# Value columns of half the recurrence units spread by DMA instead of TensorE, in units of two columns by two chunks

## The chip, the cores and the metric
The kernel runs on one core of one Trainium2 chip. A core has TensorE (PE, matrix products into PSUM), VectorE (DVE), ScalarE (ACT), GpSimd (POOL) and SyncE (SP, which here only issues DMAs). The metric is the time of one execution in microseconds, on the device; lower is better.

## The reference
The input is 32 sequences of 128 tokens of width 512. A cross-attention layer is followed by a layer with a linear recurrence (an RWKV block). The part that the change touches is the recurrence over tokens, with 32 heads of 16 keys by 16 values:

```
w = exp(-exp(time_decay + tanh(x5[1] @ decay_w1) @ decay_w2))    # per token, head and key
r, k, v = x5[3] @ Wr.T, x5[0] @ Wk.T, x5[2] @ Wv.T
def step(s, (r_t, k_t, v_t, w_t)):
    a = k_t[:, :, :, None] * v_t[:, :, None, :]                  # 16 x 16 per head
    out = einsum('bhk,bhkd->bhd', r_t, u * a + s)
    return a + w_t[:, :, :, None] * s, out
att = group_norm(outs) ; x = x + att * silu(x5[4] @ Wg.T) @ Wo.T
x = x + sigmoid(xr @ ffn_Wr.T) * (relu(xk @ ffn_Wk.T) ** 2 @ ffn_Wv.T)
```

## The kernel before
**Tiling.** Two sequences make a group of T = 256 tokens (NB = 2, L = 128), 16 groups. Width lies on partitions in 4 chunks of 128; in a chunk, a partition is one key of one of 8 heads. For each value column d (16 of them) the state of a chunk over all tokens is a row of 256 elements per partition. A unit is 4 such columns of one chunk, 128 x 1024 elements in one of four slots of the tile st; a group has 16 units, numbered by chunk.

**A unit's steps.** spread (PE, line 721): eight matmuls copy the unit's four value columns from the tiles v_hi and v_lo (v split into two float32r parts) to all 16 keys of each head, into the two-bank PSUM tile pair. outer (DVE, line 1226) multiplies it by kT into st, one token later. first (ACT, line 1031) puts the state before the first token into the element that outer leaves free. scan (DVE, line 1237) runs the recurrence, four scans of 256. weigh (DVE, line 1247) multiplies by rT. reduce (PE, line 744), for two units at a time, sums over the keys into bank 7; the bonus (line 729) is a matmul into the other half of that bank. readout (DVE, lines 1255 and 1257) adds both into att.

**Order.** Each engine is given its steps by a written order (PE_ORDER, ACT_ORDER, POOL_ORDER, DVE_ORDER) which it runs once per iteration; "+1" and "+2" mark steps that belong to the group one or two iterations back. So three groups are in work: attention and norms of one, projections and recurrence of the next, and group norm and feed-forward of the one before. low, low_rank, mix, tdecay, decay and proj_r, proj_k, proj_v, proj_g make w, r, k, v and the gate; the other PE steps are attention (score, turn_p, values, share, project) and feed-forward (ffn_k, ffn_r, ffn_v). PSUM has four further banks, used in a ring: the keys of the PE steps take them in turn, and a step waits until the bank's last reader has emptied it. Every engine executes its queue in order; a wait holds up all that stands behind it.

**SP.** turn(it) issues the loads and stores of an iteration in this order: load_c, load_s 0 and 1, store (two DMAs of 256 KB, after ffn_v), bring, load_s 2, save, load_m, load_x, load_t, load_s 3.

## Time and profile before

| | |
|---|---|
| median of 3 runs | 2274.32 us (2273.31 to 2276.19) |
| profiled execution | 2273.57 us |
| its span | 2271.8 us |
| PE / DVE / ACT / POOL busy, share of the span | 94% / 86% / 56% / 26% |
| mean granted TensorE clock | 0.97 |
| DMA moved | 69.88 MB, mean 31 GB/s |

The span is the time from the first to the last instruction of the profiled execution. Busy shares are means over the whole span, in which two iterations at either end have only part of the work; the rows below look into a steady iteration. A group of instructions is shown with its line, engine and operation, what it writes and reads, the count, the busy time in us and the mean duration of one in ns, and the idle time in front of it with its releaser.

### The profile page before, as it was taken

What the parts mean: (1) busy time and instruction counts of PE and PEld (TensorE: products, weight loads), DVE (VectorE), ACT (ScalarE), POOL (GpSimd) and SP (SyncE); (2) the same over time, 40 slices, a digit from 0 to 9 for tenths busy, and PEclk for the clock granted to TensorE, in tenths of its full rate; (3) what the DMA queues carried; (4) which work ended last, traced back from release to release, by engine and by line L of the source; (5) the groups of instructions that cost most, each with busy time, mean ns of one, the idle gap of its engine ahead of it and who ended that gap; (6) DMA issues with size and microseconds to landing.
All of it is one profiled execution on the core that took longest, in us unless ns stands there. A gap on an engine that the chain in (4) does not pass through costs nothing. (4 is left out here: it accounts for less than half of the span.)

```text
span 2271.8 us, 41733 instructions
## 1 busy us (share of the span) xinstructions
PE 2143.0 (94%) x14176; PEld 1477.1 (65%) x14176; DVE 1953.2 (86%) x4863; ACT 1260.9 (56%) x4405; POOL 585.4 (26%) x700
## 2 busy tenths in 40 slices
PE   7796999999999999999999999999999999999876
PEld 4574766667676666767667676766767676676533
DVE  2277989989898998989899898989989898998982
ACT  5555383845738384573838457383845738384312
POOL 1312232142223214222331422232142223314200
PEclk7898999999999999999999999999999999999977
DMA  8001001010010101001010100101010010100000
GB/s 282 31 20 31 2 11 50 11 50 11 16 35 11 50 11 50 11 16 36 11 50 11 50 11 14 38 11 50 11 50 11 11 41 11 50 2 29 1 19 10
DMA packets 48978, 69.88 MB, mean 31 GB/s; under 512 B 20512, under 2 KB 26656, under 8 KB 48768
## 3 DMA queue, kind: packets, MB, share of 16 engines
q1 hardware_dynamic: 48768, 67.21, 9.0%
q8 instruction: 115, 1.88, 0.4%
q14 instruction: 95, 0.78, 0.1%
HBM read 50.42 MB, written 16.78 MB: 30 GB/s over the span
## 5 line engine op out<-in xcount | busy, mean ns | idle before, releaser
L1237 DVE TENSOR_TENSOR_SCAN st<-ws,st 128x256 f32<-128x256 f32 x1024 | 637.7, 686 | 0.1
L866 ACT ACTIVATE probs_or_mixes<-probs_or_mixes,least 128x128 f32<-128x128 f32 x1024 | 399.0, 403 | 100.1 <-DVE least L1184 99.1
L1226 DVE TENSOR_TENSOR st<-bank_pair,kT 128x1016 f32<-128x1016 f32 x256 | 308.2, 1204 | 87.9 <-PE bank_pair L721 87.9
L1247 DVE TENSOR_TENSOR st<-st,rT 128x1024 f32<-128x1024 f32 x256 | 318.1, 1243 | 0.0
L1126 POOL TENSOR_SCALAR rstd<-rstd 128x1 f32<-128x1 f32 x96 | 26.6, 277 | 1099.9 <-ACT cin L899 599.9
L1184 DVE CUSTOM_DVE_ANT_0 probs_or_mixes<-bank,nmask 128x128 f32<-128x128 f32 x1024 | 231.2, 285 | 82.4 <-PE bank L568 76.8
L1120 POOL TENSOR_TENSOR probs_or_mixes<-probs_or_mixes 128x512 f32<-128x512 f32 x160 | 190.2, 1221 | 341.2 <-DVE probs_or_mixes L1278 341.2
L866 ACT ACTIVATION_READ_ACCUMULATOR probs_or_mixes<-probs_or_mixes,least 128x1 f32 x1024 | 206.7, 202 | 0.0
L721 PE MATMUL bank_pair<-v_hi,sel 32*128 32x256 f32 x1024 | 194.1, 340 | 10.6 <-DVE st L1226 10.4
L721 PE MATMUL bank_pair<-v_lo,sel 32*128 32x256 f32 x1024 | 166.8, 286 | 0.0
L721 PEld LDWEIGHTS bank_pair<-v_hi,sel 32*128 32x128 f32 x1024 | 114.4, 185 | 72.3 <-issue 35.4
L577 PE MATMUL bank<-consts,probs_or_mixes 128*128 128x128 f32 x1024 | 156.5, 285 | 3.1 <-DVE least L1184 1.5
L577 PEld LDWEIGHTS bank<-consts,probs_or_mixes 128*128 128x128 f32 x1024 | 115.8, 143 | 60.8 <-issue 38.9
L568 PE MATMUL bank<-kbd,inputs_turned 32*128 32x256 f32 x1024 | 149.5, 408 | 5.9 <-DVE least L1184 3.8
L744 PE MATMUL bank<-st,consts 128*32 128x256 f32 x2048 | 140.8, 393 | 13.7 <-DVE st L1247 13.6
L877 ACT ACTIVATE probs_or_mixes<-bank 128x512 f32<-128x512 f32 x256 | 148.9, 599 | 8.1 <-PE bank L587 4.7
L1278 DVE SCALAR_TENSOR_TENSOR probs_or_mixes<-bank,cols,probs_or_mixes 128x256 f32<-128x256 f32 x320 | 129.2, 471 | 12.2 <-PE bank L657 10.7
L613 PE MATMUL bank<-wo,probs_or_mixes 128*128 128x512 f32 x256 | 118.4, 605 | 14.2 <-DVE probs_or_mixes L1206 13.3
L1103 POOL TENSOR_TENSOR rk<-rT,kT 128x256 f32<-128x256 f32 x64 | 92.8, 1450 | 147.0 <-issue 138.9
L700 PE MATMUL bank<-probs_or_mixes,wr 128*128 128x256 f32 x512 | 119.8, 387 | 7.6 <-DVE probs_or_mixes L1278 7.5
L796 PE MATMUL bank<-last_stage,fk 128*128 128x256 f32 x512 | 120.1, 389 | 6.5 <-DVE last_stage L1339 6.5
L554 PE MATMUL bank<-inputs_turned,wq 128*128 128x256 f32 x512 | 118.5, 384 | 6.5 <-DVE least L1184 6.5
(150 smaller groups left out, 4214.3 us busy)
## 6 DMA issues: line engine op xcount, KB each, us to landing
inputs_turned<-in_ctx_turned SPq DMA_DIRECT2D x16, 512.0 KB, 3.5
inputs_turned<-in_x_turned SPq DMA_DIRECT2D x16, 512.0 KB, 4.4
xin<-in_x SPq DMA_DIRECT2D x16, 512.0 KB, 3.7
x<-xin SPq DMA_DIRECT2D x16, 512.0 KB, 4.1
keep<-x SPq DMA_DIRECT2D x16, 512.0 KB, 3.6
out<-keep SPq DMA_DIRECT2D x32, 256.0 KB, 2.0
nmask<-in_mask SPq DMA_DIRECT2D x16, 128.0 KB, 4.1
wo<-in_wo SPq DMA_DIRECT2D x2, 1024.0 KB, 12.4
```

Of the source, the lines that this page charges most:

```text
L568: last = mm(ps[m][0][:, ci * 2 * L:(ci + 1) * 2 * L], qT[r, 2 * cp + ci, b, :], kbd[r, b, :, :], start=True, stop=True)
L577: last = tr(ps[:, j * P:(j + 1) * P], pr[:, n % 4, j, :], ident)
L721: last = mm(pair[:, s, k * T:(k + 1) * T], sel[r, d % 4, :], part[r, c, :], start=part is v_hi, stop=part is v_lo)
L744: last = mm(ps[32 * (d // 4):32 * (d // 4) + 32, 0:T], ebase[:, o:o + 32], st[:, u % SLOTS, n * T:(n + 1) * T], start=m == 0 and k == 0, s ...
L866: last = fn(pr[:, n % 4, j, :], pr[:, n % 4, j, :], ACT.Exp, bias=least[:, n, j:j + 1], scale=-1.0, accum_out=rsum[:, n, j:j + 1])
L877: fn(pT[:, n % 4], ps[:].rearrange("p (j t) -> p j t", j=4), ACT.Copy).then_inc(free, 1)
L1120: tt(v, v, xnT[:, 2 * p:2 * p + 2, :, 1:], ALU.add).then_inc(mixed.sem, 1)
L1184: last = nc.vector.tensor_tensor_reduce(pr[:, n % 4, j, :], ps[:, j * P:(j + 1) * P], nmask[:, n // 8, :], 1.0, BIG, ALU.add, ALU.min, lea ...
L1226: tt(dst, src, over(kv, DU, 1), ALU.mult).then_inc(outer.sem, 1)
L1237: last = nc.vector.tensor_tensor_scan(v, ws[:, c].rearrange("p b t -> p (b t)"), v, 0.0, ALU.mult, ALU.add)
L1247: tt(v, v, over(rT[:, u // PER, :], DU, 1), ALU.mult).then_inc(weighed.sem, 1)
L1278: last = stt(out=x5[:, k % 4, c], in0=ps[:, q * T:(q + 1) * T].rearrange("p (b t) -> p b t", b=NB), scalar=col("maa", f * NC + c), in1=sx[ ...
```

## The change
A unit becomes two value columns of two chunks (again 128 x 1024 elements). UNIT_D now lists a pair of columns, eight units per pair of chunks. Units 0 to 7 (chunks 0 and 1) are spread by PE as before, in four matmuls of 512 columns. Units 8 to 15 (chunks 2 and 3) are spread by DMA: ScalarE copies that half of v as float32 to a new tile v_1, SP stores it to a DRAM tensor v_rows, and one DMA per unit reads 8 rows of 4 KB, each 16 times, straight into the unit's slot of st, one element to the right. outer then multiplies in place. Scans are two of 512 per unit; reduce works in four matmuls of 512 columns and keeps bank 7 for four steps; the bonus moves to the ring of banks. Bank 7 is freed by the new signal read_out. rk and the join of v_hi and v_lo on POOL are done for two chunks at once, the join for units 0 to 7 alone. SP gets a written order too, and the orders of all engines are new.

```diff
+HALF_T = 2 * T
+UNIT_D = [(4 * (w % 2) + w // 2, 8 + 4 * (w % 2) + w // 2) for w in range(2 * PER)]
+PITCH = DU * T + 4
+BY_PE = UNITS // 2
 PE_ORDER = """
+reduce.4+2 low_rank.0+1 reduce.5+2 key.0 tdecay.0+1 low_rank.2+1 value.0 proj_r.0+1 proj_v.0+1 proj_k.0+1 decay.0+1
+spread.0+1 reduce.6+2 decay.1+1 reduce.7+2 spread.1+1 query.0 var.0+2 proj_r.1+1 score.0 spread.2+1 rstd.0+2 query.1
...
+score.14 turn_p.11 project.0 turn_m.1+2 turn_p.12 reduce.3+1 values.2 flip.1 turn_p.13 turn_p.14 turn_p.15 share.1
+values.3 project.1 ffn_k.0+2 ffn_k.1+2 ffn_r.0+2 ffn_r.1+2 turn_n.0 turn_n.1 ffn_v.0+2 ffn_v.1+2 low.0
 """
 ACT_ORDER = """
+low.0+1 first.12+2 state.0+1 key.0 tdecay.0+1 state.1+1 first.13+2 first.14+2 proj_v.0+1 first.15+2 proj_k.0+1
...
 """
 DVE_ORDER = """
+scan.12+2 mix.2+1 mix.3+1 outer.13+2 value.0 scan.13+2 outer.14+2 outer.15+2 scan.14+2 weigh.12+2 proj_v.0+1
...
+inverse.0 scan.5+1 outer.6+1 weigh.4+1 scan.6+1 weigh.5+1 score.10 score.11 weigh.6+1 outer.7+1 score.12 score.13
+gather.0 scan.7+1 score.14 score.15 weigh.7+1 outer.8+1 outer.9+1 project.0 inverse.1 readout.0+1 shift2.0+2
+outer.10+1 gather.1 scan.8+1 outer.11+1 project.1 scan.9+1 scan.10+1 scan.11+1 weigh.8+1 weigh.9+1 shift.0 weigh.10+1
+ffn_v.0+2 weigh.11+1 ffn_v.1+2 mix.0 mix.1 outer.12+1
 """
+SP_ORDER = """
+load_c.0 load_s.0+1 load_s.1+1 save_v.1+2 spread.8+2 spread.9+2 load_m.0 spread.10+2 spread.11+2 save.0+1 load_x.0
+load_t.0 store.0+3 spread.12+2 spread.13+2 spread.14+2 spread.15+2 bring.0+2 load_s.2+1 load_s.3+1
+"""
...
+            def save_v(g, _):
+                wait(sp, outer.sem, outer.after(g, 0))
+                key = ("proj_v", 1)
+                sp.wait_ge(emptied[XB.of(key)], XB.through(key, g))
+                for half in range(2):
+                    sp.dma_start(v_rows[:, half], v_1[64 * half:64 * half + 64, :, :]
+                                 .rearrange("p c n -> p (c n)")).then_inc(v_saved.sem, 16)
...
+                sp.wait_ge(v_saved.sem, v_saved.after(g, 2))
+                wait(sp, summed.sem, summed.after(g, (u - SLOTS) // 2 + 1))
+                r = HC * UNIT_D[u % (2 * PER)][0]
+                src = v_rows[r:r + HC].rearrange("h s n -> h (s n)")
+                sp.dma_start(st[:, u % SLOTS, 1:DU * T + 1],
+                             src.unsqueeze(1).to_broadcast([HC, HD, DU * T])).then_inc(landed[u % SLOTS].sem, 16)
...
             def spread(g, u):
+                wait(pe, outer.sem, outer.after(g, u) if u else outer.after(g - 1, BY_PE))
+                for part in (v_hi, v_lo):
+                    for half in range(2):
+                        d = UNIT_D[w][half]
+                        r = slice(32 * (d // 4), 32 * (d // 4) + 32)
+                        last = mm(pair[:, half, :], sel[r, d % 4, :],
+                                  part[r, :, :].rearrange("p c n -> p (c n)"),
+                                  start=part is v_hi, stop=part is v_lo)
...
             def reduce(g, q):
+                p, m = q // PER, q % PER
                 if m == 0:
+                    wait(pe, read_out.sem, read_out.after(g, p))
+                if m == PER - 1:
+                    bonus(g, p)
...
+                for half in range(2):
                     for u in (2 * q, 2 * q + 1):
+                        r = 64 * half + 32 * (u % 2)
+                        last = mm(bank[7][r:r + 32, :], ebase[:, o:o + 32],
+                                  st[:, u % SLOTS, half * HALF_T:(half + 1) * HALF_T], start=m == 0, stop=m == PER - 1)
...
             def first_state(g, u):
+                if u < BY_PE:
+                    wait(act, summed.sem, summed.after(g, (u - SLOTS) // 2 + 1))
+                else:
+                    v_there(act, g, u)
...
             def outer_(g, u):
+                if u < BY_PE:
+                    wait(dve, summed.sem, summed.after(g, (u - SLOTS) // 2 + 1))
+                    dve.wait_ge(spreaded.sem, spreaded.after(g, u + 1))
+                    src = pair[:].rearrange("p s (r t) -> p s r t", t=L)[:, :, :, 0:L - 1]
+                else:
+                    v_there(dve, g, u)
+                    src = dst
...
             def scan(g, u):
+                for half in range(2):
+                    v = st[:, u % SLOTS, half * HALF_T:(half + 1) * HALF_T]
```

v_there waits for the landing of the unit's own DMA.

## Rows read from the trace of the kernel before

**Rows 1.** DVE in order of time, value's sum in two groups: start us, us, instruction.
```profile
253.13 0.47 DVE L1172 TENSOR_TENSOR vpad<-bank,rows 128x128 f32<-128x128 f32 x2
...
1976.90 0.47 DVE L1172 TENSOR_TENSOR vpad<-bank,rows 128x128 f32<-128x128 f32 x2
```
**Rows 2.** Stretch, length; busy PE, PEld, DVE, ACT, POOL; clock, DMA share, GB/s.
```profile
651.10:783.70 132.60, 130.81 (x885) 90.66 (x885) 121.64 (x305) 78.37 (x275) 36.30 (x44) 1.00 0.08 26
...
1976.90:2100.00 123.10, 119.54 (x793) 82.46 (x793) 112.14 (x291) 74.33 (x264) 33.48 (x41) 1.00 0.04 14
```
**Rows 3.** Waits from 651.1 to 1049: waiter, releaser, us, times, longest.
```profile
DVE st L1226 <- PE bank_pair L721: 16.1, 6, 4.9
```
**Rows 4.** Busy time of one line alone in a period: spread (721), then reduce (744).
```profile
651.10:783.70 132.60, 14.33 (x128) 10.55 (x128) 1.00 0.08 26
651.10:783.70 132.60, 8.54 (x128) 3.44 (x128) 1.00 0.08 26
```
**Rows 5.** PE in order of time: one spread and the step behind it.
```profile
737.38 0.38 PE L721 MATMUL bank_pair<-v_hi,sel 32*128 32x256 f32 x2
...
738.04 1.12 PE L804 MATMUL bank<-fr,last_stage 128*128 128x512 f32 x2
```
**Rows 6.** Groups of VectorE by line and form: busy us, mean ns, idle before.
```profile
L1237 DVE TENSOR_TENSOR_SCAN st<-ws,st 128x256 f32<-128x256 f32 x1024 | 637.7, 686 | 0.1
L1247 DVE TENSOR_TENSOR st<-st,rT 128x1024 f32<-128x1024 f32 x256 | 318.1, 1243 | 0.0
L1226 DVE TENSOR_TENSOR st<-bank_pair,kT 128x1016 f32<-128x1016 f32 x256 | 308.2, 1204 | 87.9 <-PE bank_pair L721 87.9
L1257 DVE TENSOR_TENSOR att<-bank,dg 128x256 f32<-128x256 f32 x64 | 27.2, 424 | 2.2
L1339 DVE SCALAR_TENSOR_TENSOR last_stage<-last_stage,cols 128x256 f32<-128x256 f32 x128 | 52.0, 478 | 10.4 <-ACT last_stage L1039 10.4
L1287 DVE TENSOR_TENSOR v_lo<-bank,v_hi 128x512 fp32r<-128x512 f32 x32 | 21.5, 672 | 6.8 <-ACT v_hi L983 6.7
```
**Rows 7.** DMA issues: queue, count, KB each, median us from issue to landing.
```profile
inputs_turned<-in_ctx_turned SPq DMA_DIRECT2D x16, 512.0 KB, 3.5
inputs_turned<-in_x_turned SPq DMA_DIRECT2D x16, 512.0 KB, 4.4
out<-keep SPq DMA_DIRECT2D x32, 256.0 KB, 2.0
wq<-in_wq SPq DMA_DIRECT2D x1, 1024.0 KB, 7.6
```
**Rows 8.** DVE in order of time, mix.0 and mix.1.
```profile
754.56 3.22 DVE L1278 SCALAR_TENSOR_TENSOR probs_or_mixes<-bank,cols,probs_or_mixes 128x256 f32<-128x256 f32 x8
```
**Rows 9.** SP's queue in order of time, the two stores of a group.
```profile
750.56 2.81 SPq L441 DMA_DIRECT2D out<-keep  x2
```
**Rows 10.** PE and ACT around the boundary, in order of time.
```profile
751.25 1.54 ACT L956 ACTIVATE th<-bank 32x256 f32<-32x256 f32 x4 [6.36 <-PE bank L643]
755.57 1.97 PE L533 MATMUL bank<-inputs_turned,wk 128*128 128x256 f32 x8
757.47 1.07 PE L744 MATMUL bank<-st,consts 128*32 128x256 f32 x16
...
760.19 0.38 PE L721 MATMUL bank_pair<-v_hi,sel 32*128 32x256 f32 x2
760.77 1.89 PE L657 MATMUL bank<-th,w2s 32*128 32x256 f32 x16
763.12 2.18 PE L700 MATMUL bank<-probs_or_mixes,wr 128*128 128x256 f32 x9 [0.46 <-DVE probs_or_mixes L1278]
```
**Rows 11.** PE alone by half microseconds: busy, clock, where it stood still early in the run.
```profile
149.50:150.00 0.50, 0.18 (x2) 1.00 0.00 0
...
152.50:153.00 0.50, 0.37 (x3) 0.89 0.04 16
...
159.50:160.00 0.50, 0.50 (x9) 0.78 0.00 0
```

More of the change, by code:

```diff
@@ L121 @@
 PE_ORDER = """
-reduce.4+2 spread.12+2 low_rank.0+1 spread.13+2 key.0 reduce.5+2 tdecay.0+1 spread.14+2 low_rank.2+1 proj_r.0+1
-spread.15+2 decay.0+1 proj_v.0+1 proj_k.0+1 spread.0+1 reduce.6+2 decay.1+1 value.0 spread.1+1 reduce.7+2 query.0
-spread.2+1 var.0+2 proj_r.1+1 score.0 rstd.0+2 query.1 score.2 spread.3+1 proj_g.0+1 proj_g.1+1 turn_p.0 turn_p.1
-turn_p.2 reduce.0+1 spread.4+1 score.4 out.0+2 turn_p.3 score.6 spread.5+1 turn_p.4 out.1+2 values.0 reduce.1+1
-turn_p.5 score.8 spread.6+1 proj_v.1+1 turn_p.6 flip.0 proj_k.1+1 turn_p.7 turn_m.0+2 score.10 share.0 spread.7+1
@@ L156 @@
-scan.7+1 inverse.1 project.0 weigh.7+1 outer.9+1 shift2.0+2 gather.1 scan.8+1 project.1 outer.10+1 readout.1+1
-weigh.8+1 scan.9+1 outer.11+1 weigh.9+1 scan.10+1 scan.11+1 shift.0 weigh.10+1 ffn_v.0+2 weigh.11+1 ffn_v.1+2
-"""
+scan.12+2 mix.2+1 mix.3+1 outer.13+2 value.0 scan.13+2 outer.14+2 outer.15+2 scan.14+2 weigh.12+2 proj_v.0+1
+weigh.13+2 scan.15+2 weigh.14+2 weigh.15+2 outer.0+1 mix.4+1 readout.1+2 outer.1+1 scan.0+1 var.0+2 score.0 outer.2+1
+score.1 groupnorm.0+2 scan.1+1 outer.3+1 score.2 weigh.0+1 proj_g.0+1 score.3 weigh.1+1 scan.2+1 proj_g.1+1 weigh.2+1
@@ L495, in _ @@
             for it in range(G + LATEST):
-                turn(it)
+                for name, n, late in SP_STEPS:
+                    g = it - late
+                    if known(g) and not (g == 0 and name in FIRST):
+                        does[name](g, n)
             sp.wait_ge(stored.sem, stored.after(G, 0))
@@ L705, in spread @@
             def spread(g, u):
-                c = u // PER
                 if first_group(g) and u == 0:
@@ L710, in spread @@
                     pe.wait_ge(sel_ready, 1)
-                if u % (2 * PER) == 0:
-                    key = ("proj_v", u // (2 * PER))
+                if u == 0:
+                    key = ("proj_v", 0)
                     pe.wait_ge(emptied[XB.of(key)], XB.through(key, g))
-                wait(pe, outer.sem, outer.after(g, u))
-                for k in range(2):
-                    for part in (v_hi, v_lo):
-                        for s in range(2):
-                            d = UNIT_D[u % PER][2 * s + k]
-                            r = slice(32 * (d // 4), 32 * (d // 4) + 32)
-                            last = mm(pair[:, s, k * T:(k + 1) * T], sel[r, d % 4, :], part[r, c, :],
-                                      start=part is v_hi, stop=part is v_lo)
@@ L731, in reduce, with bonus @@
+                last.then_inc(spreaded.sem, 1)
+            def bonus(g, p):
+                pe.wait_ge(rk_done.sem, rk_done.after(g, p + 1))
+                ps, full = y_bank(("bonus", p), g)
+                for q in range(2):
+                    last = mm(ps[:, q * T:(q + 1) * T], ublk[:, 2 * p + q, :], rk[:, q, :], start=True, stop=True)
+                last.then_inc(full, 1)
             def reduce(g, q):
-                m, c = q % 2, q // 2
+                p, m = q // PER, q % PER
                 if m == 0:
-                    bonus(g, c)
+                    wait(pe, read_out.sem, read_out.after(g, p))
+                if m == PER - 1:
+                    bonus(g, p)
@@ L1222, in outer_ @@
[L1222 to L1226 removed]
+                dst = st[:, u % SLOTS, 0:DU * T].rearrange("p (s r t) -> p s r t", s=2, t=L)[:, :, :, 1:]
```

252 lines of the change are left out of this document (115 added, 137 removed).

## The prediction

> **What bounds the kernel now.** I read the page's busy shares first, then the period, then the waits inside a period. A group's value projection is added up on VectorE at 253.13 us for one group and at 1976.90 us for the thirteenth after it [rows 1]: (1976.90 - 253.13) / 13 = 132.6 us per group, so the steady part decides. In such a period TensorE is busy for 130.8 of 132.6 us, VectorE for 121.6, ScalarE for 78.4, GpSimd for 36.3, and TensorE's granted clock is 1.00 [rows 2], its upper level, 2.4 GHz. TensorE idles 1.8 us per period. VectorE idles 11, and the longest of its waits is for TensorE: in three periods 16.1 us in front of the outer products, for the spread [rows 3]. So TensorE's queue is the bound, with VectorE 9 us behind it. A change is worth what it takes off TensorE, until VectorE or a chain of waits is the next.
>
> **TensorE, removed and reshaped.** Eight of sixteen spreads per group leave TensorE. By busy time the sixteen cost 14.33 us [rows 4], 0.90 each, but neighbours overlap. Start to start one costs less: its first matmul starts at 737.38 and the next step's at 738.04 [rows 5], 0.66 us. Eight fewer give 8 x 0.66 = 5.3 us; the busy time would give 7.2. I take 5.3, because the period is made of starts. The eight that stay are 4 matmuls of 512 columns instead of 8 of 256: the same columns, fewer starts. The eight old ones start some 0.08 us apart (0.66 / 8), the two halves still lie in different row strips, and I take 0.6 us per group off. If the halves did not overlap when wide, each would cost some 0.3 us more, 2.4 us per group. The sums over the key rows (line 744) cost 8.54 us per group for eight steps [rows 4]; four wide matmuls instead of eight narrow ones in four column strips, the same columns, I take 0.5 us off, bounds 0 and 1.5. The bonus keeps its matmuls and moves to every fourth sum. TensorE: 5.3 + 0.6 + 0.5 = 6.4 us per period off, bounds 3 and 10.
>
> **VectorE.** 64 scans of 256 become 32 of 512. A scan takes 686 ns, a plain product of the same size 424, one of 1024 1243 ns [rows 6]: the slope of the products is (1243 - 424) / 768 = 1.07 ns per element and their fixed part some 150 ns. With that fixed part a scan costs (686 - 150) / 256 = 2.1 ns per element, a wide one 1.22 us, and each pair saves one fixed part less the overlap of neighbours (637.7 us / 1024 = 623 ns against 686, 63 ns): some 90 ns, 32 x 0.09 = 2.9 us, bounds 0 and 4.8. The read-out is 4 products of 512 (0.67 each by the v_lo row) for 8 of 256 (0.42): 0.7 us less. One v_lo subtraction goes, 0.7. The outer product of a unit that DMA spreads reads st in SBUF instead of the PSUM pair, as the product with r does: 1243 x 1016 / 1024 for 1204 ns, 8 x 0.03 = 0.2 us more. VectorE: 4.1 us less, 117.5. That is still under TensorE's 130.8 - 6.4 = 124.4, so none of it shortens the period by itself; it pays for new waits. GpSimd joins half as much of v and ScalarE's copies only change their target; both have idle time for it.
>
> **DMA, added.** Per group 2 stores of 128 KB and 8 spreads of 512 KB come to 4.4 MB; the kernel moves 26 GB/s, 3.4 MB per period, with a DMA share of 0.08 [rows 2], so the share goes to some 0.18 and the volume is free. The latency is not: spread.u waits in SP's queue for the sum that frees its slot, and for everything ahead of it. A 512 KB load lands 3.5 to 4.4 us after issue, a 1024 KB one 7.6, a 256 KB store 2.0 [rows 7]. Per pair of units:
> - Units 8 and 9 need reduce.2 and the stores of v. On VectorE some ten steps, about 14 us, lie between weigh.5 and outer.8: hidden.
> - Units 10 and 11 need reduce.3, which needs weigh.7. Behind it come read-out and shift2 (8 products of 478 ns [rows 6], less their overlap some 3.4 us) before outer.10. About 1 us can show on VectorE, whose slack covers it: the next step that TensorE needs is the shift, which waits for the chain of norms, and the new order leaves it only three scans and two products before that.
> - Units 12 and 13 are the tight ones. On SP, spread.12 stands behind the store of the group before, which waits for the last step of ffn_v. In the trace the second of these stores is issued at about 753.0 and SP is free at 750.56 + 2.81 = 753.4 [rows 9]. On VectorE only mix.0 and mix.1, 3.2 us [rows 8], lie before outer.12. scan.12, and behind it mix.2 and mix.3, queue behind outer.12, and TensorE's value and proj_r need banks that mix.2 empties.
> - Units 14 and 15 follow in the same queue, while VectorE has mix.2, mix.3, value and a scan to do: hidden.
>
> **The boundary, step by step.** TensorE ends low at 751.2 and has a bonus, a sum and a spread as cover until tanh is done at 751.25 + 1.54 = 752.8 [rows 10]. The sum alone reaches 752.2: 0.6 us idle. Then, by [rows 10], low_rank.0 1.9, key 1.9, a sum and tdecay 2.7 (757.47 to 760.19), low_rank.2 1.9: 761.2 at value. VectorE ends mix.1 at about 757.2. spread.12 is issued at 753.4 with half a megabyte of stores ahead of it, of which the second is just out: 4.4 + 1.6 = 6.0 us, lands at 759.4. The bounds are 3.5 and 7.6 us, 756.9 and 761.0; I take 6.0 since it is the nearest row with the same bytes per partition plus most of the store's 2.0. Then outer.12 1.1, scan.12 2.3, first half of mix.2 0.9: 763.7, so TensorE idles 2.5 us where it idled 0.46 [rows 10]: 2.0 us more. By the bounds it is -0.4 and 3.6.
>
> **DMA engines.** Every load of the trace has 128 partitions as its outermost dimension; the spread's source has 8. The page "DMA: Bandwidth & Descriptors" of the Trainium skill (section on why a DMA increments its semaphore by 16) says that a transfer runs on the largest number of engines, at most 16, that divides the outermost dimension of both sides, which would be 8 here. By that rule each engine carries as much as in the 1024 KB row, and the period would end at 132.6 - 6.4 + 0.6 + 3.6 = 130.4 us, not 128.8, the whole near 2241 us. No row of before shows such a transfer.
>
> **The sum.** 132.6 - 6.4 + 0.6 + 2.0 = 128.8 us, 3.8 less. Fourteen periods from 121.8 to 1976.9 give 53 us. The next iteration, which still has TensorE at 119.5 of 123.1 us [rows 2], gives 3. The last 172 us run a chain of one group's tail, in which narrow steps and DMA latency exchange; I leave it at 0 (bounds -8 and +8). The profiled execution took 2273.57 us with a span of 2271.8; 2273.6 - 56 = 2217.6. The median of the runs is 0.7 above it: **2218 us**.
>
> **The rivals.**
> - **Landing is hidden, TensorE sheds more.** The overlap that I gave away in the spread comes back (7.2 + 0.6 + 0.5) and spread.12 lands by 758: 132.6 - 8.3 + 0.6 + 0.4 = 125.3 us; 14 x 7.3 + 5 = 107, 2167 us. If only the landing is early, 126.8, 2186. For it: the busy time of rows 4. Against it: the store ahead of spread.12. Chance 0.26 for both.
> - **The boundary lets the clock fall.** The trace has such a place in its first periods: TensorE stands still from about 149.7 to 152.6 us, and the granted clock is at 0.50, the lower level of 1.2 GHz, from 152.9 to 159.7 [rows 11], 6.8 us of which half are lost, 3.4 us. Landing after 7.6 us makes the gap at value 2.5 + 1.6 = 4.1 us, and in every period: 132.6 - 6.4 + 0.6 + 3.6 + 3.4 = 133.8 us, 14 x 1.2 + 1 = 18 us slower, 2292 us. It decides from a gap of at most 2.9 us, as in that stretch; my forecast has 2.5, so it is near. For it: SP's order and a source of 8 rows. Against it: key, tdecay and low_rank.2 keep TensorE busy right before. Chance 0.22, and if the clock falls in every second period only, the time is near 2265.
> - **The work does not leave TensorE.** If wide halves do not overlap (2.4 us back) and the landing takes 7.6 us, 132.6 - 4.0 + 0.6 + 3.6 = 132.8: no change, 2274. Chance 0.08.
>
> The page "TensorE: Matmul & The Clock Gate" (section on what is happening) says that an array left idle is let have half of its clock pulses, and the trace agrees, with 0.50 after the stop in rows 11; by that rule a long enough gap gives the second rival's 2292.
>
> **How the numbers follow.** Forecast 0.44 (2190 to 2245 for its own bounds), the rivals 0.26, 0.22, 0.08. The range takes in the first rival but for its far end and the second: 2160 to 2295. This kernel can be told from no change at about 0.2%, 4.5 us. Faster: 0.44 + 0.26 and a little of the others, 0.73; within: 0.07; slower: 0.20.
>
> **What will show it.** In a steady period: TensorE's busy time near 124 us; a spread with 4 matmuls some 0.6 us start to start; wide scans at about 1.2 us; DMA share about twice; VectorE's wait before the outer product naming a DMA at unit 12, of 2 to 3 us; the landing of the 512 KB spreads, 4.4 or 7.6; TensorE's wait at value and the granted clock behind it. The prediction is wrong if ScalarE, whose first.12 now waits for the landing ahead of key, holds up more than value, or if other DMA waits fall on TensorE's path.

## The result and the profile after

The change made the kernel slower: 2439.76 us (2435.67 to 2443.24, 4 runs) against 2274.02 beside it, ratio 1.0724, 95% interval 1.0712 to 1.0737. The sign of the prediction was wrong and the time lies 145 us above its range. The profiled execution took 2443.24 us, its span is 2441.0.

The page after: busy times; the groups that answer to [rows 6]; the DMAs (count, KB each, median us to landing, where there is one).
```profile
PE 2165.6 (89%) x11616; PEld 1421.2 (58%) x11616; DVE 1961.5 (80%) x4271; ACT 1270.2 (52%) x4405; POOL 553.9 (23%) x620
...
L1272 DVE TENSOR_TENSOR_SCAN st<-ws,st 128x512 f32<-128x512 f32 x512 | 638.5, 1288 | 94.9 <-ACT st L1061 94.3
...
L1261 DVE TENSOR_TENSOR st<-st,kT 128x1016 f32<-128x1016 f32 x128 | 178.5, 1400 | 147.5 <-DMA st<-v_rows 147.5
L1061 ACT ACTIVATE st<-s 128x8 f32<-128x8 f32 x256 | 52.3, 210 | 237.0 <-DMA st<-v_rows 233.2
L1261 DVE TENSOR_TENSOR st<-bank_pair,kT 128x1016 f32<-128x1016 f32 x128 | 154.1, 1204 | 4.7 <-PE bank_pair L738 4.7
```
VectorE waits 147.5 us for landings and 94.3 us for ScalarE's first states, ScalarE itself 233.2 us for the same landings. The wide scans cost together what the narrow ones did, 638.5 against 637.7 us [rows 6]; the section on why the prediction was wrong takes this sum apart.

Marks of the period, as in [rows 1], then one steady period in the columns of [rows 2], with the spread (line 738) and the reduce (763) alone.
```profile
242.46 0.48 DVE L1204 TENSOR_TENSOR vpad<-bank,rows 128x128 f32<-128x128 f32 x2
...
2105.00 0.47 DVE L1204 TENSOR_TENSOR vpad<-bank,rows 128x128 f32<-128x128 f32 x2
```
```profile
1100.71:1244.33 143.62, 133.59 (x725) 87.81 (x725) 122.85 (x268) 78.88 (x275) 34.19 (x39) 0.94 0.21 55
...
1100.71:1244.33 143.62, 6.38 (x32) 2.80 (x32) 0.94 0.21 55
...
1100.71:1244.33 143.62, 8.50 (x64) 1.36 (x64) 0.94 0.21 55
```
(2105.00 - 242.46) / 13 = 143.3 us per group, 10.7 more than before; the window above is 11.0 more. TensorE idles 10.0 us of it where it idled 1.8 [rows 2], 8.2 more. It is busy 2.8 us longer though it has less to do, because a part of it runs at the lower clock: in a run further down (short landings, changed order) the same work takes 126.65 us at a clock of 1.00. So, by that run, the work shrank by about 130.8 - 126.7 = 4.1 us and the clock costs about 133.6 - 126.7 = 6.9: 8.2 + 6.9 - 4.1 = 11.0.

Where TensorE waits, three periods after (columns as in [rows 3]).
```profile
PE bank L614 <- DVE rinv L1229: 11.7, 3, 3.9
PE bank L677 <- ACT low_b L982: 9.3, 3, 3.4
...
```
There are two stops per period, each with a landing behind it. The other waits are of 0.9 us and less. **Stop A** is at flip.1, the end of attention. In order of time, SP's issues, VectorE and TensorE:
```profile
1175.55 0.63 SPq L477 DMA_DIRECT2D st<-v_rows  x1
...
1182.72 1.22 DVE L1261 TENSOR_TENSOR st<-st,kT 128x1016 f32<-128x1016 f32 x1 [1.88 <-DMA st<-v_rows]
...
1186.89 1.22 DVE L1261 TENSOR_TENSOR st<-st,kT 128x1016 f32<-128x1016 f32 x1 [2.95 <-DMA st<-v_rows]
1189.03 0.41 PE L614 MATMUL bank<-consts,rinv 128*32 128x128 f32 x2 [3.93 <-DVE rinv L1229]
```
spread.8 is issued at 1175.55 and lands at 1182.7, 7.2 us later; spread.9, issued 0.7 us behind it, lands 4.2 us behind it. outer.8 and outer.9 stand ahead of inverse.1 on VectorE, and flip.1 needs inverse.1.

**Stop B** is at low_rank.2, between two groups.
```profile
1227.87 1.29 SPq L477 DMA_DIRECT2D st<-v_rows  x2
...
1235.15 0.22 ACT L1061 ACTIVATE st<-s 128x8 f32<-128x8 f32 x1 [8.34 <-DMA st<-v_rows]
1235.15 1.22 DVE L1261 TENSOR_TENSOR st<-st,kT 128x1016 f32<-128x1016 f32 x1 [3.78 <-DMA st<-v_rows]
1238.14 1.97 PE L677 MATMUL bank<-th,w2s 32*128 32x256 f32 x8 [3.40 <-ACT low_b L982]
```
spread.12 takes 1235.15 - 1227.87 = 7.3 us. ScalarE's first.12 waits for it ahead of state, key and tdecay, and low_rank.2 needs tdecay. VectorE waits 1.88, 2.95 and 3.78 us for units 8, 9 and 12 in this period, and not at all for 10, 11 and 13 to 15. Behind both stops the granted clock falls. TensorE alone by 4 us: busy, clock, DMA share, GB/s.
```profile
1184.00:1188.00 4.00, 1.11 (x20) 1.00 0.51 128
...
1192.00:1196.00 4.00, 3.12 (x23) 0.50 0.25 62
1196.00:1200.00 4.00, 4.00 (x5) 0.50 0.00 0
...
1236.00:1240.00 4.00, 1.86 (x8) 0.79 0.54 119
1240.00:1244.00 4.00, 4.00 (x19) 0.50 0.53 127
```
While spreads alone are moving, the DMA share is 0.51 and the rate 128 GB/s; 512 KB at that rate are 4.1 us, the 4.2 between two landings. The spread itself:
```profile
1112.38 0.50 PE L738 MATMUL bank_pair<-v_hi,sel 32*128 32x512 f32 x2
...
1113.04 1.07 PE L763 MATMUL bank<-st,consts 128*32 128x512 f32 x8
```
1113.04 - 1112.38 = 0.66 us from start to start with four wide matmuls, what eight narrow ones took [rows 5].

### The profile page after: what moved, and what is told of

It reads as the page before. It is cut to its first block, busy times and chain, and to the rows that moved or that the text cites. A ratio compares the mean times of both kernels' runs of the same rounds, so it can differ in the third digit from the quotient of the medians.

```text
span 2441.0 us, 35975 instructions
## 1 busy us (share of the span) xinstructions
PE 2165.6 (89%) x11616; PEld 1421.2 (58%) x11616; DVE 1961.5 (80%) x4271; ACT 1270.2 (52%) x4405; POOL 553.9 (23%) x620
## 4 chain that ended last, share of the span: by engine, by line
PE 63%; DMA 13%; DVE 12%; ACT 7%; issue 4%; SPq 1%; POOL 1%; DVEq 0%; POOLq 0%; ACTq 0%
PE bank L718 18%; DMA st<-v_rows 12%; PE bank L814 5%; PE bank L573 5%; PE bank L795 4%; PE bank L596 4%; PE bank L632 4%; DVE st L1283 4%; PE bank L587 4%; PE bank L763 3%; DVE st L1272 3%; PE bank L822 3%; PE bank_pair L738 3%; PE bank L561 2%; PE bank L606 2%
## 5 line engine op out<-in xcount | busy, mean ns | idle before, releaser
L1272 DVE TENSOR_TENSOR_SCAN st<-ws,st 128x512 f32<-128x512 f32 x512 | 638.5, 1288 | 94.9 <-ACT st L1061 94.3
L1261 DVE TENSOR_TENSOR st<-st,kT 128x1016 f32<-128x1016 f32 x128 | 178.5, 1400 | 147.5 <-DMA st<-v_rows 147.5
L1061 ACT ACTIVATE st<-s 128x8 f32<-128x8 f32 x256 | 52.3, 210 | 237.0 <-DMA st<-v_rows 233.2
L587 PE MATMUL bank<-kbd,inputs_turned 32*128 32x256 f32 x1024 | 168.1, 405 | 4.1 <-DVE least L1216 2.7
L763 PE MATMUL bank<-st,consts 128*32 128x512 f32 x1024 | 138.6, 614 | 35.3 <-DVE st L1283 35.2
L632 PE MATMUL bank<-wo,probs_or_mixes 128*128 128x512 f32 x256 | 147.4, 729 | 25.1 <-DVE probs_or_mixes L1238 13.3
L1261 DVE TENSOR_TENSOR st<-bank_pair,kT 128x1016 f32<-128x1016 f32 x128 | 154.1, 1204 | 4.7 <-PE bank_pair L738 4.7
L587 PEld LDWEIGHTS bank<-kbd,inputs_turned 32*128 32x128 f32 x1024 | 107.6, 188 | 39.3 <-issue 27.6
L677 PE MATMUL bank<-th,w2s 32*128 32x256 f32 x512 | 79.5, 443 | 57.3 <-ACT low_b L982 46.1
L814 PEld LDWEIGHTS bank<-last_stage,fk 128*128 128x128 f32 x512 | 100.9, 197 | 37.3 <-DVE last_stage L1380 16.7
```

Of the source, the lines that this page charges most:

```text
L587: last = mm(ps[m][0][:, ci * 2 * L:(ci + 1) * 2 * L], qT[r, 2 * cp + ci, b, :], kbd[r, b, :, :], start=True, stop=True)
L632: last = mm(ps[:], oT[:, b, c, :], wo[:, c, :], start=c == 0, stop=c == NC - 1)
L763: last = mm(bank[7][r:r + 32, :], ebase[:, o:o + 32], st[:, u % SLOTS, half * HALF_T:(half + 1) * HALF_T], start=m == 0, stop=m == PER - 1)
L814: last = mm(ps[:, q * T:(q + 1) * T], big["fk"][:, e, c * P:(c + 1) * P], xk[:, e], start=e == 0, stop=e == NC - 1)
L1261: tt(dst, src, over(kv, 2, 1), ALU.mult).then_inc(outer.sem, 1)
L1272: last = nc.vector.tensor_tensor_scan(v, ws[:, 2 * p:2 * p + 2].rearrange("p c b t -> p (c b t)"), v, 0.0, ALU.mult, ALU.add)
```

## The experiments

Each edit is against the kernel after. Steps are named as in the orders. All times are medians of at least four executions, ratios are to the kernel before, which stood at 2273.5 to 2275.8 us beside them, with the 95% interval in brackets.

### Is it the landing?

**Short transfers.** The transfers keep their places, and most of their length goes. Seven eighths of a slot keep old numbers, so this run leaves out a part of the computation; it is only there for its time.
```diff
-sp.dma_start(st[:, u % SLOTS, 1:DU * T + 1], src.unsqueeze(1).to_broadcast([HC, HD, DU * T]))
+sp.dma_start(st[:, u % SLOTS, 1:1 + 128], src[:, 0:128].unsqueeze(1).to_broadcast([HC, HD, 128]))
```


> The changed kernel with the same DMAs in the same places on the same number of engines, but each spread moves 128 of the 1024 elements (512 B per partition); the other 896 elements of a slot are left as they are, so the recurrence of units 8 to 15 is computed from other numbers. Theory A (the length of the landing makes both stops): landing 2.5 to 3.5 us, no wait of VectorE for units 9 and 12 above 1 us, clock near 1.00, period 129 to 133, time 2220 to 2290 us. Rival C (orders and units): above 2340 us, as the kernel with all spreads on TensorE (2348).

2274.59 us, ratio 0.9999 [0.9989, 1.0009]: 165 us less than after. VectorE's wait for DMA falls from 147.5 to 3.9 us. So the length of the transfers makes the whole 165 us, and theory A holds. But the gain that was predicted does not come either: 133.0 us per period, where the sum had 128.8.

**Sixteen rows.** SP stores each row of v twice, so that a spread's source has 16 rows of 4 KB, each read 8 times.
```diff
-src = v_rows[r:r + HC].rearrange("h s n -> h (s n)")
-... src.unsqueeze(1).to_broadcast([HC, HD, DU * T])
+src = v_rows[r:r + HC].rearrange("h k s n -> (h k) (s n)")
+... src.unsqueeze(1).to_broadcast([2 * HC, HD // 2, DU * T])
```


> Every row of v is stored twice in DRAM, so that the source of a spread has 16 rows in its outermost dimension instead of 8 (the stores grow from 128 to 256 KB each). Theory A (the spreads run on half of the DMA engines, one lands 7.2 us after issue and the next 4.2 us later, and the two stops of TensorE per period come from that): landing near 4 us, the next about 2 us later, DMA share in those stretches near 1.0 instead of 0.5, both stops shrink below 2 us and the clock stays at 1.00; period from 143.3 to about 130, 2440 to about 2240 us. Rival B (the source is slow because each row is read 16 times, or because of the element offset, not because of the number of engines): landing stays near 7 us and the time within 1% of 2440. Rival C (the wide units and the new orders cost the time, DMA is incidental): landing falls, the time stays above 2380.

2298.14 us, ratio 1.0098 [1.0081, 1.0116]: 142 us less than after, 58 more than expected, so the mechanism held and the size of the rest did not. A 4 us window with spreads in flight, and the page's line of the same transfer:
```profile
1028.44:1032.44 4.00, 2.32 (x19) 1.00 1.03 232
```
```profile
L1262 DVE TENSOR_TENSOR st<-st,kT 128x1016 f32<-128x1016 f32 x128 | 167.5, 1319 | 36.2 <-DMA st<-v_rows 35.9
```
The share is 1.03 and the rate 232 GB/s, where 8 rows gave 0.51 and 128. (One other load is in this stretch; from 978 to 980 us, with spreads alone, the share is 1.04 and the rate 268.) That agrees with the rule of the Trainium skill that the prediction named, "DMA: Bandwidth & Descriptors", section on why a DMA increments its semaphore by 16: 8 engines against 16. With it the first landing of a pair takes 4.7 to 4.8 us instead of 7.2 to 7.3 (in two runs further down, 1029.42 to 1034.07 and 1020.39 to 1025.18).

### Can stop B be ordered away?

**ScalarE's first.12 behind key and tdecay.**
```diff
-low.0+1 first.12+2 state.0+1 key.0 tdecay.0+1 state.1+1 first.13+2
+low.0+1 state.0+1 key.0 tdecay.0+1 first.12+2 state.1+1 first.13+2
```


> The changed kernel with one edit: on ScalarE first.12 stands behind key and tdecay. Transfers as they are. If the stop at low_rank.2 comes from ScalarE's queue (first.12 waits 8.3 us for the landing, key and tdecay behind it, and TensorE waits 3.4 us for low_b): the stop shrinks, but VectorE's outer.12 still lands at the same time and mix.2 behind it becomes the releaser: 1 to 3 us per period less, 2440 to between 2390 and 2425. If ScalarE's queue alone made it: 2440 to about 2370.

2439.44 us, no effect, where 2390 to 2425 was expected. The wait at low_rank.2 is gone and stands at value:
```profile
PE bank L561 <- DVE probs_or_mixes L1321: 10.4, 3, 3.7
```
value needs mix.2, which is behind outer.12 on VectorE, as the prediction had it. ScalarE hid the wait that VectorE has anyway. With 16 rows the same edit does nothing either:

> Rows stored twice (16 engines, landing 4.8 us for unit 12, time 2298) and first.12 behind key and tdecay. In the kernel with 16 engines alone VectorE's outer.12 waits 1.25 us and ScalarE's first.12 5.8 us. If ScalarE's queue is what is left of the stop: the clock falls once per period at most, period 134.6 to 131, time near 2245. If VectorE's own wait is: 2290 to 2300.

2301.58 us, ratio 1.0123 [1.0108, 1.0138], against 2298.14.

**outer.12 and scan.12 behind mix.3 and value too,** with ScalarE's first.12 behind state.1.
```diff
-ffn_v.0+2 weigh.11+1 ffn_v.1+2 mix.0 mix.1 outer.12+1
-scan.12+2 mix.2+1 mix.3+1 outer.13+2 value.0 scan.13+2
+ffn_v.0+2 weigh.11+1 ffn_v.1+2 mix.0 mix.1
+mix.2+1 mix.3+1 value.0 outer.12+2 scan.12+2 outer.13+2 scan.13+2
```


> Transfers as in the changed kernel (8 engines). VectorE takes outer.12 and scan.12 behind mix.2 and mix.3, ScalarE takes first.12 behind key, tdecay and state.1. The one place is the boundary, where VectorE's own queue had the wait of 3.8 us for the landing ahead of mix.2; moving only ScalarE's step left the time at 2439. Theory A (in-order queue behind the landing): that stop of TensorE and its half clock go, 5 to 7 us per period, 2440 to 2335 to 2370. Rival E (the other stop grows by as much, because VectorE has no slack): above 2410.

2442.67 us, ratio 1.0738 [1.0722, 1.0754]. The wait has moved once more, to spread.0:
```profile
PE bank_pair L738 <- DVE v_lo L1329: 11.8, 3, 4.0
```
v_lo now stands behind outer.12 to outer.15. The landing took 3.4 us from TensorE at low_rank.2, 3.7 at value, 4.0 at spread.0: in all three orders something that TensorE needs stands behind the late step. The expectation, 2335 to 2370, was missed; its rival E holds.

### Can stop A be ordered away?

**VectorE's project.0, inverse.1 and gather.1 ahead of the outer products that wait for a landing.**
```diff
-weigh.7+1 outer.8+1 outer.9+1 project.0 inverse.1 readout.0+1 shift2.0+2
-outer.10+1 gather.1 scan.8+1 outer.11+1 project.1 scan.9+1
+weigh.7+1 project.0 inverse.1 outer.8+1 readout.0+1 shift2.0+2
+gather.1 outer.9+1 scan.8+1 outer.10+1 project.1 outer.11+1 scan.9+1
```


> Transfers as in the changed kernel. VectorE takes project.0 and inverse.1 ahead of outer.8, gather.1 right behind shift2 and outer.9 behind that, so that no step which TensorE waits for stands behind the landing of units 8 to 10. Theory A: the stop before flip.1 (3.9 us) and its half clock go, 5 to 7 us per period, 2440 to 2335 to 2370. The kernel with three orders moved gave 2378 and still stopped 4.0 us at project.1, because outer.9 and outer.10 stood ahead of gather.1: if that was the reason, this one has no stop above 1.5 us there. Rival E: above 2410.

2337.33 us, ratio 1.0273 [1.0258, 1.0288]: 102 us less than after, as theory A had it. Stop A is gone from the waits, stop B stays:
```profile
PE bank L677 <- ACT low_b L982: 9.5, 3, 3.3
```
**A half way there** was tried first: project.0 and inverse.1 ahead of outer.8, gather.1 left behind outer.10, with spread.12 and 13 ahead of the store on SP and the ScalarE edit above.

> Written orders only, transfers as in the changed kernel: on SP spread.12 and spread.13 ahead of the store; on ScalarE first.12 behind key and tdecay; on VectorE project.0 and inverse.1 ahead of outer.8 and outer.9. Theory A with the landing as it is: the steps behind the waits no longer wait for the DMA; the stop at flip.1 (3.9 us) goes, the one at low_rank.2 (3.4 us) shrinks, since outer.12 still stands ahead of scan.12 and mix.2; the clock falls at most once per period: 143.3 to 132 to 137 us per period, 2440 to 2270 to 2345. Rival C: no change, since the waits are only where the time is counted. Rival D (the landing is set by SP's order, behind the store): spread.12 lands in 4 to 5 us after issue instead of 7.2.

2378.05 us, ratio 1.0458 [1.044, 1.0475], above the 2270 to 2345 that were expected: the stop of 4.0 us is at project.1, which needs gather.1. With 16 rows as well:

> Rows stored twice and the three changes of order together (spread.12 and spread.13 ahead of the store, first.12 behind tdecay, project.0 and inverse.1 ahead of outer.8 and outer.9). Theory A: the landing and the queues behind it are the whole loss; TensorE's work is 5 us under that of before, so the period goes to 128 to 130 and the time to 2205 to 2240, faster than before. If it ends above 2275, a part of the loss lies in the new orders apart from these places.

2317.36 us, ratio 1.019 [1.0175, 1.0205], slower than 16 rows alone, though VectorE's wait for DMA is down to 5.8 us in the whole span. By the expectation's own words, a part of the loss lies in the orders.

**All orders together**, with 8 and with 16 rows: the edit of stop A above, the edit that put outer.12 behind value, and spread.12 and 13 ahead of the store on SP.

> Both orders of the last two together, and spread.12 and spread.13 ahead of the store on SP; 8 engines. Theory A: landing of 7 us hidden everywhere, both stops gone: 2240 to 2290 us. If the clock still falls once per period from stops of about 1 us (as in the kernel with short transfers, 2275), 2270 to 2300.

> The same orders with rows stored twice (16 engines). If the landing no longer matters once nothing urgent stands behind it, this is within 1% of the kernel with 8 engines; if it still does (slots free later, units 10 and 14), 1 to 3% faster. Theory A gives 2200 to 2260 us, under the kernel before (2274), since TensorE has 5 us less work per period.

2356.78 and 2345.30 us, ratios 1.036 and 1.0307, both far above what was expected. Both have a period of 138.0 us, and with 16 rows VectorE waits for DMA only 4.3 us in the whole span. So in these orders the transfer is no longer the cause; the order is:
```profile
PE bank_pair L739 <- DVE v_lo L1330: 11.0, 3, 3.7
```

### Is it the clock, and does DMA pay at all?

**Filling the stops** with three useless matmuls of 512 columns ahead of low_rank.2 and of flip.1:

> Three matmuls of 512 columns (0.85 us each) with no use, into the idle bank pair, right before low_rank.2 and again right before flip.1, the two places where TensorE stops for 3 to 4 us per period. Nothing of the computation is left out. If the clock that falls after each stop costs its share (mean clock 0.945 of 143.3 us, 7.9 us per period), filling the stops keeps it at 1.00 in them: period near 136 us, time 2320 to 2350. If the fall of the clock is only where the profile shows it and costs nothing, the time is the same or up to 1% longer (2.6 us each, in waits of 3.4 and 3.9 us).

2412.25 us, ratio 1.0593 [1.0565, 1.0621], above the 2320 to 2350 that were expected. The clock in a period rises from 0.94 to 1.00 and 0.98 in the two looked at, and only 27 us of the median come back (43 in the profiled execution, 2399.81 us) of the 6.9 x 14 = 97 that the low clock seemed to cost. The filling itself takes 2.8 us at each stop, and what TensorE does faster it then waits for, 2.3 us at project.1.

**All sixteen spreads by TensorE** in the new units, with no transfer (an order patched by hand, with spread.8 to 15 put back into TensorE's order, so this run mixes two things):

> The new units (two columns by two chunks), wide scans, sums and read-out, but all 16 spreads by TensorE, no v_rows and no spread by DMA; orders of the changed kernel with the spreads put back. Theory A: this is the changed kernel without its cause: TensorE's work is that of before less about 1 us, VectorE's less 4: 128 to 134 us per period, 2220 to 2300 us, clock 1.00 in steady periods. Rival C (units and orders cost the time): above 2380 us.

2348.53 us, ratio 1.0324 [1.0309, 1.034], period 137.1, TensorE busy 132.6 at a clock of 1.00. No spread by DMA is in it and it is still 74 us slower than before, between what theory A and rival C had. It can't tell whether the units or the patched order cost that.

### What holds the period once landings are covered?

**Both repairs**, 16 rows and the order that took stop A away:

> Both changes that helped alone: v rows stored twice so that a spread's source has 16 rows outermost (alone 2298 us), and VectorE's project.0 and inverse.1 ahead of outer.8, gather.1 right behind shift2 (alone 2337 us). Theory A (the stop at the end of attention is the order of VectorE's queue, and what is left of the loss after the shorter landing is that stop): the stop of TensorE in front of project.1 and flip.1 that 16 rows alone still show goes, the period falls from 134.6 by 1.5 to 4 us, to 130.6 to 133.1, time 2240 to 2280 us. Rival B (what is left is the boundary, where spread.12 stands between two groups): the stop at attention goes but a longer one at value or low_rank.2 takes its place, period within 0.7 us of 134.6, time 2288 to 2308.

2307.06 us, ratio 1.0141 [1.0126, 1.0156]. Rival B's end: 142 and 102 us do not add up, and together they are 9 us worse than 16 rows alone. **The same with spread.12 and 13 ahead of the store on SP:**
```diff
-load_t.0 store.0+3 spread.12+2 spread.13+2 spread.14+2
+load_t.0 spread.12+2 spread.13+2 store.0+3 spread.14+2
```


> The first kernel of this call (16 rows, VectorE's order at the end of attention) with spread.12 and spread.13 also ahead of the store on SP. Theory A (the store ahead of spread.12 costs at the boundary, as the prediction put it): 0.5 to 1.5 us per period less than the first kernel of this call, 8 to 20 us less in all. Rival B (spread.12 waits for the sum that frees its slot, not for SP, or its landing is not what TensorE waits for): within 5 us of that kernel.

2281.41 us, ratio 1.0028 [1.0017, 1.0038]: 26 us less, where theory A had 8 to 20. In the run without it SP issues the stores, then the spread; with it spread.12 goes out first and lands before VectorE stands at outer.12:
```profile
1026.52 2.80 SPq L455 DMA_DIRECT2D out<-keep  x2
1029.42 3.09 SPq L478 DMA_DIRECT2D st<-v_rows  x4
...
1034.07 1.22 DVE L1262 TENSOR_TENSOR st<-st,kT 128x1016 f32<-128x1016 f32 x1 [1.34 <-DMA st<-v_rows]
```
```profile
1020.39 1.17 SPq L478 DMA_DIRECT2D st<-v_rows  x2
1021.61 1.05 SPq L455 DMA_DIRECT2D out<-keep  x2
...
1025.18 0.22 ACT L1062 ACTIVATE st<-s 128x8 f32<-128x8 f32 x1 [4.32 <-DMA st<-v_rows]
```
From issue to landing spread.12 takes 4.65 us with the stores in front of it and 4.79 without. So the store costs the time that SP spends on it, and not time of the landing. That it costs was right in the prediction, and this is the fastest version with the whole computation that I found; it doesn't beat the kernel before. **Short transfers with the order of stop A:**

> The spread DMAs move 128 of their 1024 elements per partition (the rest of the slot is left as it is), with VectorE's order of the end of attention changed as in the run with project.0 and inverse.1 ahead of outer.8. It shows what the change could give if landings cost nothing. Short transfers alone gave 2274.6 us, with TensorE busy for 127.7 of 133.0 us. Theory A (the 5.3 us that are left idle there lie at the end of attention): period 129 to 131.5, time 2215 to 2255, and the 5.3 us of the spreads are earned. Rival B (the idle time comes from the new order at the boundary): period 132 to 133.5, 2262 to 2280.

2279.38 us, ratio 1.0022 [1.0012, 1.0031]: rival B in period and nearly in time (like the other run with short transfers, this one leaves out a part of the computation). Its period:
```profile
897.50:1030.81 133.31, 126.65 (x726) 82.99 (x725) 123.50 (x267) 78.56 (x275) 40.61 (x39) 1.00 0.11 32
```
With landings almost free and a full clock TensorE is busy 126.65 us and idles 6.7, nearly all of it in eight waits of 0.33 to 1.53 us: for ScalarE, VectorE and GpSimd. Before, in three periods, there are three kinds, 1.6 us per period together:
```profile
PE bank L613 <- DVE probs_or_mixes L1206: 2.6, 3, 0.9
PE bank L700 <- DVE probs_or_mixes L1278: 1.4, 3, 0.5
PE bank L554 <- DVE least L1184: 0.8, 3, 0.3
```
**Filling the two waits of 0.9 us** at value and project.1 in the best version, with two and with four useless matmuls:

> The best kernel so far (16 rows, VectorE's order at the end of attention, spread.12 and 13 ahead of the store on SP; 2281 us) with two useless matmuls of 512 columns (0.43 us) ahead of value and two ahead of project.1, where TensorE waits 0.93 and 0.88 us and the granted clock falls behind the wait. Theory A (the fall of the clock, 0.015 to 0.02 of a 133.3 us period, is what keeps it behind the kernel before): the clock stays at 1.00, the matmuls lie in time that was idle, period 131 to 132, time 2248 to 2266 us, below the kernel before. Rival B (the waits keep their places because the chain of the order is what counts, not TensorE's speed): the clock stays up but the idle time grows by as much, 2275 to 2285.

> The same with four matmuls in each place (0.85 us, the length of the wait). Theory A: as with two, 2248 to 2270 us; if two are too few to keep the clock, only this one gains. Rival B: 2278 to 2292, since the filling now runs past the wait.

2282.60 and 2301.49 us, ratios 1.0037 and 1.0125. The filling was longer than the expectations say: each matmul of 512 columns runs as two instructions, and two matmuls hold TensorE for 1.8 us (989.38 to 991.20), four for 3.5 (903.44 to 906.98), where the waits were 0.9. Even so, with two the clock is at 1.00, TensorE is busy 130.0 us, and the period is the same:
```profile
900.91:1034.25 133.34, 129.96 (x733) 84.52 (x733) 123.38 (x268) 78.64 (x275) 40.63 (x39) 1.00 0.23 61
```
Four in each place lengthen it by 1.2 us, to 134.5. So in the best version TensorE is not the bound. **Taking two waits of VectorE away**, 3.53 and 1.67 us per period, in the best version:
```diff
-first.9+1 apply0.0 norm0.1 ffn_k.0+2 apply0.1 keep_row.0 norm1.0
-first.10+1 norm1.1 row1.0 ffn_r.0+2 apply1.0 first.11+1 apply1.1
+first.9+1 apply0.0 norm0.1 ffn_k.0+2 first.10+1 first.11+1 apply0.1 keep_row.0 norm1.0
+norm1.1 row1.0 ffn_r.0+2 apply1.0 apply1.1
```


> The kernel with 16 rows, VectorE's order at the end of attention and spread.12 and 13 ahead of the store (2281 us, period 133.3), with ScalarE's first.10 and first.11 moved ahead of the second apply0 (before, behind norm1.0 and norm1.1, which wait for GpSimd). There VectorE's scan.10 waits 3.53 us and scan.11 1.67 us for them in every period, though outer.10 and outer.11 were done 6 us earlier. Theory A (the period of 133.3 us, the same with TensorE's clock at 1.00 or 0.98 and with 128 or 130 us of its work, is a chain through VectorE's queue, and these two waits are in it): VectorE gets up to 5.2 us back, TensorE's waits at value, proj_r and project.1 shrink, period 129 to 131.5, time 2218 to 2256 us, faster than the kernel before. Rival B (the waits are cover that something later eats, such as VectorE's wait for the shift or ffn_v of the group behind): the 5.2 us come back as idle time of VectorE elsewhere, period 132.8 to 133.6, 2272 to 2286.

2330.47 us, ratio 1.0245 [1.0228, 1.0263], period 136.7: worse than either theory, 49 us slower than the version it changes. Three stretches in order of time, GpSimd's part in the chain of norms for the second half of a group. Before, where VectorE waits 4.93 us for the spread:
```profile
736.07 0.55 POOL L1128 TENSOR_TENSOR rstd<-rstd,mhalf 128x1 f32<-128x1 f32 x1
...
738.22 1.22 DVE L1226 TENSOR_TENSOR st<-bank_pair,kT 128x1016 f32<-128x1016 f32 x1 [4.93 <-PE bank_pair L721]
```
The best version, then the one with the two waits taken away:
```profile
1003.12 1.27 POOL L1147 TENSOR_TENSOR xin<-xin,rows 128x512 f32<-128x512 f32 x1
...
1005.54 1.39 POOL L1161 TENSOR_TENSOR rstd<-rstd,mhalf 128x1 f32<-128x1 f32 x1
1007.01 0.19 POOL L1164 TENSOR_TENSOR less<-less,rstd 128x1 f32<-128x1 f32 x1
```
```profile
1017.67 7.72 DVE L1273 TENSOR_TENSOR_SCAN st<-ws,st 128x512 f32<-128x512 f32 x5
...
1022.24 2.06 POOL L1147 TENSOR_TENSOR xin<-xin,rows 128x512 f32<-128x512 f32 x1
...
1025.45 1.46 POOL L1161 TENSOR_TENSOR rstd<-rstd,mhalf 128x1 f32<-128x1 f32 x1
1026.99 0.70 POOL L1164 TENSOR_TENSOR less<-less,rstd 128x1 f32<-128x1 f32 x1
...
1029.76 0.44 PE L643 MATMUL bank<-consts,inputs_turned 128*128 128x128 f32 x2 [3.38 <-ACT inputs_turned L925]
```
The same GpSimd instruction takes 0.55 us while VectorE is still and 1.39 to 1.46 beside scans. With scans back to back the chain from apply0 to turn_n grows from 1009.3 - 1000.89 = 8.4 us to 1029.76 - 1020.00 = 9.8, and the three GpSimd lines above (2.06 for 1.27, 0.70 for 0.19, 1.46 for 1.39) are that growth. TensorE waits 3.38 us at turn_n, and VectorE waits 6.08 us for the shift behind it. So VectorE's waits were in part GpSimd's time. They are not the whole of it: the stop at turn_n is longer than the growth also because TensorE comes there earlier, with project.1 and what follows up to ffn_r done in 17.2 us at a clock of 1.00 (1009.20 to 1026.38) and not in 18.9 at 0.91 (990.31 to 1009.18 in the best version).

## Why the prediction was wrong, point by point

The sum said 128.8 us for a period, and the period looked at has 143.6. Of the 14.8 us between them TensorE's work makes 2.3 (4.1 us less and not 6.4), the clock 6.9, and idle time 5.6 (10.0 us where the sum had 1.8 + 0.6 + 2.0).

- **The bound and the price of landings.** That TensorE's queue bounds the kernel held for before. The forecast's own term for a landing was 6.0 us, between bounds of 3.5 and 7.6. It is 7.3. The bound of the 1024 KB row was the right one, and the rule of the Trainium skill that the prediction named ("DMA: Bandwidth & Descriptors", section on why a DMA increments its semaphore by 16) pointed at it; choosing the nearer row by bytes per partition was the mis-sized term. Its parts were wrong as well: spread.8, with no store ahead of it, takes 7.2 us and not 4.4, and the 1.6 us for the stores in the queue are not there (4.65 us with them, 4.79 without, at 16 rows). But the right length alone would have given 130.4 us, not 143.3.
- **Units 8 and 9, "about 14 us ... hidden".** This is the step that failed most. I counted VectorE's steps from weigh.5, which reduce.2 needs, and not from when TensorE gets to reduce.2. weigh.5 ends at 1169.3 and VectorE stands at outer.8 at 1182.72 - 1.88 = 1180.84, 11.5 us later. But the sum stands far down TensorE's queue and ends at 1175.4, right before the issue at 1175.55, so the DMA had 5.3 us for a landing of 7.2. Stop A, 3.9 us and the clock behind it, was worth 102 us of the 165 (order run).
- **12 and 13, the boundary.** The mechanism was right: outer.12 waits for the landing, value behind it, and the store ahead of it costs (26 us). VectorE's wait was 3.78 us where "2 to 3" was named. The first to stop was low_rank.2, through ScalarE's first.12, which the prediction gave as what would make it wrong; the run that moved it shows that this route adds nothing, since VectorE's is as long.
- **The clock.** The rival had the mechanism, in one place and with a gap of at most 2.9 us. There are two places with 3.9 and 3.4, and it costs 6.9 us of TensorE's time where 3.4 were set. It falls earlier too: in the run with short transfers the granted clock is 0.60 from 987.2 to 991.2 us, right behind a stop of 1.30 us, while the other run with short transfers has a stop of 1.53 us and stays at 1.00 behind it. The filling runs show that its fall follows the stops and is mostly not the cause of the time: only 27 us came back.
- **TensorE, -6.4 us.** It was 4.1. The 0.6 and 0.5 for wide spreads and sums are not there: 0.66 us each as before, and 8.50 for 8.54 us of sums. Nor are the 5.3 us of the spreads there in full. The prediction priced one that stands alone, 0.66 us. Some stood inside a score step: the two together take 667.13 - 665.60 = 1.53 us in the kernel before, where a score alone takes 1.06, so such a spread was worth 0.5 us. What makes up the rest of the 1.2 us that are missing was not traced.
- **VectorE, -4.1 us.** It came out at +1.2 (121.64 to 122.85). The wide scans do save something, as long as GpSimd is still: two of them take 2.33 us where four narrow ones took 2.43.
```profile
674.42 2.43 DVE L1237 TENSOR_TENSOR_SCAN st<-ws,st 128x256 f32<-128x256 f32 x4
```
```profile
1106.18 2.33 DVE L1272 TENSOR_TENSOR_SCAN st<-ws,st 128x512 f32<-128x512 f32 x2
```
That is 0.10 us per unit and 1.6 per group, where 2.9 were set. But the scans of a unit that have a GpSimd instruction beside them (104 of 256 units) take 2.74 us on average, where the narrow ones took 2.63 (95 of 256), and the totals come out equal, 638.5 and 637.7. In the best version it is 112 units with 3.03 us, and 674.1 us in all, 2.3 more per group than before. The outer product from SBUF costs 1.217 us in the median, as it was set; but where GpSimd works beside it (31 of 128) it takes 2.00, which makes the mean of 1.400. The prediction said of GpSimd only that it has idle time, and put nothing for what the two engines cost each other. So the slack that was to pay for new waits was smaller by 5 us.
- **The gain itself.** Even with landings almost free (2274.6 us) none of the 53 us appears. The prediction took 1.8 us of idle time as given and added to it; the idle time is a property of the order, and the new order has 5.3 to 6.7. How much of that comes from VectorE and GpSimd standing in each other's way, and how much from other short waits, is open: no run has the new units in the old order, or scans of 256 in the new units.

Of the rivals, the second (clock) named the right direction with a ninth of the size, 18 us of 165. The condition of the third did not come true: wide halves overlap, or a spread would take more than 0.66 us; they only save nothing.

## What to carry to other kernels

For each transfer that replaces an engine's work, find when its last precondition really runs in the trace, on the engine whose queue holds it, and count the slack from there; steps of another engine are no measure. Set a landing's length by rows outermost and the share of DMA engines, not by bytes. And before counting a bound engine's saving as the period's, check that another chain isn't as long: here the three fastest versions came to 133 us with 127 to 130 us of TensorE's work, and others whose VectorE waits for DMA as little came to 136 and 138, by their orders. Last, look behind a mean: the median of an instruction and what runs beside its slowest ones say whether its form or its neighbour costs the time.

## What the runs showed of the hardware

- **Rows outermost.** 8 rows: share 0.51, 128 GB/s, 7.2 to 7.3 us for the first of a pair, 4.2 more for the next. 16 rows: share 1.03 to 1.04, 232 to 268 GB/s, 4.7 to 4.8 us for the first.
- **GpSimd beside VectorE.** In the kernel after, an outer product with both inputs in SBUF starts while GpSimd works, and the next GpSimd instruction starts while the outer product works:
```profile
1198.01 2.21 DVE L1261 TENSOR_TENSOR st<-st,kT 128x1016 f32<-128x1016 f32 x1
```
```profile
1197.88 1.26 POOL L1144 TENSOR_TENSOR xin<-xin,rows 128x512 f32<-128x512 f32 x1 [0.93 <-ACT xin L924]
1199.23 2.12 POOL L1146 TENSOR_TENSOR xin<-xin,rows 128x512 f32<-128x512 f32 x1
```
The outer product ends at 1200.22, 1.08 us after the first GpSimd instruction, and the second GpSimd one ends at 1201.35, 1.13 us after the outer product: each ends about as if it had begun when the other ended. Undisturbed they take 1.21 and 1.27. Over the whole trace this outer product takes 1.21 us without a GpSimd instruction beside it (97 of 128) and 2.00 with one (31), while the form that reads the PSUM pair takes 1.20 and 1.21 and never more than 1.22. The Trainium skill says in "SBUF — State Buffer", section on the two separate sides, that VectorE and GpSimd share a pair of ports under a lock, held for the whole instruction, and that a VectorE instruction with two inputs in SBUF is one that takes it. The traces agree, in both directions and for both forms of the outer product.
- **What decides how often they meet is the order.** The GpSimd instruction of one element per partition (rstd, 96 in a run) has a median of 0.55 us in the kernels before and after and in the best version. Its mean is 755 ns before, 699 after, and 943 to 956 in every version with the order that takes stop A away, with 8 rows or 16: there 46 of the 96 take more than 1.2 us, before 16, after 17. Whether the wide scans alone, in an unchanged order, make GpSimd wait longer wasn't tried.
- **Long columns save little or nothing.** Scans: 2.33 us for two of 512 against 2.43 for four of 256, without GpSimd beside them. Row- and column-tiled matmuls: 0.66 us against 0.66 for the spread, 8.50 against 8.54 for the sums.
